# An attention layer and a routed mixture of experts on one core: the side work of the attention's 16 slots assigned anew

## The reference

```python
# layer 1: attention with 16 heads of 16, weights scaled by a "coherence" and mixed with a field
attn = softmax(q @ k.T / sqrt(16))
coh = sigmoid(tanh(concat(x, cond) @ Wc1.T + bc1) @ Wc2.T + bc2)
mod = attn * coh;  mod = mod / (mod.sum(-1) + 1e-8)
mod = 0.79 * mod + 0.21 * field          # one field weight for each key, from the condition
x = x + (mod @ v) @ Wout.T + bout
# layer 2: 8 experts of three products each, the best two for each row
gate = softmax(rmsnorm(x) @ wg_W + wg_b + cond @ gg_W + gg_b)
cw = the two largest gates of each row, zero elsewhere
x = x + sum over experts of cw * (W3 . relu(W2 . relu(W1 . x + b1) + b2) + b3)
```

## Time and profile before

| | us |
|---|---|
| median of 3 runs | 947.46 (939.85, 947.46, 947.79) |
| the profiled execution | 939.21 |
| its span | 937.1 |
| PE busy | 875.0 (93%) |
| DVE busy | 700.6 (75%) |
| ACT busy | 582.2 (62%) |
| POOL busy | 405.7 (43%) |

### The profile page before, as it was taken

The page is one execution under the profiler, slowest core; times in us unless marked ns, Lnnn a source line. Parts: engine busy times, 40 slices in busy tenths (PEclk is TensorE's granted clock), DMA queues, the critical chain, the costliest instruction groups (busy, mean ns, idle before and its releaser), DMA issues.

```text
span 937.1 us, 23130 instructions
## 1 busy us (share of the span) xinstructions
PE 875.0 (93%) x6806; PEld 513.9 (55%) x6807; DVE 700.6 (75%) x1678; ACT 582.2 (62%) x1256; POOL 405.7 (43%) x446
## 2 busy tenths in 40 slices
PE   5799999999999999998988889999999999999994
PEld 2233333333333333332321568888888888888873
DVE  7888889898889989898887578667855555555542
ACT  3267787887877788776577767644444444444441
POOL 4414345545656456552343436534642332223322
PEclk9899999999999999998796999999999999999998
DMA  6462261633616254360046489435643333333442
GB/s 220 114 105 71 50 115 55 108 98 88 126 60 107 93 102 89 82 129 5 20 148 220 145 222 254 85 54 107 125 78 47 57 52 53 46 48 58 69 45 24
DMA packets 109434, 88.39 MB, mean 94 GB/s; under 512 B 63816, under 2 KB 102088, under 8 KB 107024
## 3 DMA queue, kind: packets, MB, share of 16 engines
q1 hardware_dynamic: 95664, 68.05, 31.6%
q0 software_dynamic: 13296, 18.23, 11.7%
q10 hardware_dynamic: 384, 0.97, 0.3%
HBM read 45.01 MB, written 33.31 MB: 84 GB/s over the span
## 4 chain that ended last, share of the span: by engine, by line
PE 74%; DVE 9%; DMA 6%; ACT 5%; issue 3%; POOL 1%; SPq 1%; ACTq 0%; DVEq 0%; POOLq 0%
PE bank L1025 28%; PE bank L870 11%; PE bank L922 9%; PE bank L1041 9%; PE bank L857 8%; DVE mx L1290 4%; PE bank L846 4%; DMA raw<-in_we 3%; PE bank L928 2%; ACT arena L1173 2%; PE bank L980 1%; DVE arena L1596 1%; POOL arena L626 1%; DMA out<-y,y_dest 1%; ACT arena L1121 1%
## 5 line engine op out<-in xcount | busy, mean ns | idle before, releaser
L1290 DVE TENSOR_REDUCE mx<-bank 128x1 f32<-128x512 f32 x512 | 324.2, 682 | 40.8 <-PE bank L846 37.5
L1173 ACT ACTIVATE arena<-bank 128x512 f32<-128x512 f32 x512 | 277.5, 596 | 64.8 <-PE bank L857 63.6
L1209 ACT ACTIVATE hf<-bank,small 128x256 f32<-128x256 f32 (+1 forms) x312 | 133.5, 455 | 187.9 <-PE bank L1025 183.7
L725 POOL DMA_INDIRECT out<-y,y_dest x71 | 123.2, 1735 | 240.4 <-DVE y_dest L1577 212.4
L1025 PE MATMUL bank<-hh,arena 128*128 128x256 f16 (+1 forms) x1248 | 198.4, 264 | 0.0
L1558 DVE TENSOR_TENSOR hl<-hf,hh 128x256 f16<-128x256 f32 (+1 forms) x304 | 112.8, 396 | 99.0 <-ACT hh L1213 98.8
L846 PE MATMUL bank<-arena 48*128 48x512 f16 x512 | 170.4, 394 | 14.3 <-DVE mx L1290 12.3
L857 PE MATMUL bank<-arena 49*128 49x512 f16 x512 | 166.6, 398 | 12.6 <-ACT arena L1173 6.9
L1025 PE MATMUL bank<-hl,arena 128*128 128x256 f16 (+1 forms) x624 | 163.5, 263 | 0.0
L870 PE MATMUL bank<-arena 128*17 128x512 f32 x1024 | 142.5, 630 | 0.9 <-ACT arena L1173 0.9
L857 PEld LDWEIGHTS bank<-arena 49*128 49x128 f16 x512 | 38.9, 94 | 178.5 <-ACT arena L1173 150.2
(11 more groups left out here) (230 smaller groups left out, 987.9 us busy)
## 6 DMA issues: line engine op xcount, KB each, us to landing
raw<-in_we SPq DMA_DIRECT2D x16, 1024.0 KB, 5.3
arena<-parts_dram SPq DMA_DIRECT2D x84, 128.0 KB
parts_dram<-arena SPq DMA_DIRECT2D x64, 128.0 KB, 1.8
arena<-in_xT SPq DMA_DIRECT2D x8, 512.0 KB, 4.5
arena<-in_x SPq DMA_DIRECT2D x8, 512.0 KB, 6.3
out<-rows SPq DMA_DIRECT2D x8, 512.0 KB, 5.2
xs<-in_pads SPq DMA_DIRECT2D x9, 272.0 KB, 3.8
arena<-parts_dram SPq DMA_DIRECT2D x24, 64.0 KB, 2.8
```

The costliest lines, as they stand in the source:

```text
L725: pool.indirect_dma_start(out=out, out_offset=bass.IndirectOffsetOnAxis(ap=y_dest[:, par, s:s + 1], axis=0), in_=y[:, par, s, :], in_offse ...
L1173: nc.scalar.activation(pr[:, s % TT, n, :], b_bank[no % B_RING][:, :], ACT.Exp, scale=SCALE).then_inc(b_read, 1)
L1209: nc.scalar.activation(hf[which][:, m, 0:n], layer[which][m // 2][:, m % 2 * TS:m % 2 * TS + n], ACT.Relu, bias=bias[which][:, bass.ds(e, ...
L1290: V.tensor_reduce(mx[:, g % 2, c, s % TT:s % TT + 1], a_bank[no % A_RING][:, :], X, ALU.max).then_inc(a_read, 1)
```

## The change

Only tables and the places of calls change; every instruction stays.

- `at` 0 (the first half of the second turning) of a batch moves from slot 11 to slot 0 of the next batch (in the last batch, to slot 13).
- `v` 0 moves from slot 0 to slot 4, `v` 2 from 14 to 13, `vs` from 7 to 6 and GpSimd's `sum_values` from 6 to 5.
- `pj` 3 moves from slot 13 to 14; its write to DRAM from 15 to 16, ahead of the first stack read, which moves from slot 0 to 1.
- `split_x` moves from slot 4 to 1 on ScalarE and from 5 to 2 on GpSimd.
- `square_rows` 0 moves from slot 4 to 5. `send_high` moves from slots 8 and 9 to 6 and 9, `send_low` from 8 and 10 to 7 and 14, `targets` from 14 to 15.

```diff
 PLAN = {
-    0: [("coh", 0, 0), ("v", 0, 1)],
+    0: [("at", 0, -1), ("coh", 0, 0)],
...
-    4: [("op", 1, -1)],
+    4: [("op", 1, -1), ("v", 0, 1)],
     5: [("ot", 0, 0), ("op", 2, -1)],
-    6: [("op", 3, -1)],
-    7: [("vs", 0, 0), ("c1", 0, 1)],
+    6: [("op", 3, -1), ("vs", 0, 0)],
+    7: [("c1", 0, 1)],
...
-    11: [("at", 0, 0), ("v", 1, 1)],
+    11: [("v", 1, 1)],
     12: [("pj", 1, 2), ("count", 0, -1)],
-    13: [("ot", 2, 0), ("pj", 3, 2)],
-    14: [("v", 2, 1)],
+    13: [("ot", 2, 0), ("v", 2, 1)],
+    14: [("pj", 3, 2)],
...
-SENT_AT = {8: 0, 10: 1}
+SENT_HIGH_AT = {6: 0, 9: 1}
+SENT_AT = {7: 0, 14: 1}
+SQUARES_AT = {5: (0, 1), 6: (2,), 7: (3,)}
...
-STACKS_AT = {0: 0, 3: 1, 4: 2}
+STACKS_AT = {1: 0, 3: 1, 4: 2}
...
-PARTS_AT = (10, 12, 14, 15)
+PARTS_AT = (10, 12, 14, 16)
...
+    if s == FINAL + 13:
+        here.append(("at", 0, B - 1))
...
+            if at == PARTS_AT[3] - SLOTS and 0 <= b + 1 < B:
+                write_parts(3, b + 1)
...
-            if at in PARTS_AT and 0 <= b + 2 < B:
+            if at in PARTS_AT[:3] and 0 <= b + 2 < B:
...
-            if at == 5 and 0 < b + 2 < B:
+            if at == 2 and 0 < b + 2 < B:
                 split_x(b + 2)
-            if at == 6 and 0 <= b < B:
+            if at == 5 and 0 <= b < B:
                 sum_values(b)
...
-            if at == 14 and 0 <= b - 1 < B:
+            if at == 15 and 0 <= b - 1 < B:
                 targets(b - 1)
...
-            if 4 <= at < 8 and 0 <= b - 1 < B:
-                square_rows(at - 4, b - 1)
-            if at in (8, 9) and 0 <= b - 1 < B:
-                send_high(at - 8, b - 1)
+            if at in SQUARES_AT and 0 <= b - 1 < B:
+                for t in SQUARES_AT[at]:
+                    square_rows(t, b - 1)
+            if at in SENT_HIGH_AT and 0 <= b - 1 < B:
+                send_high(SENT_HIGH_AT[at], b - 1)
...
-            if at == 4 and 0 < b + 2 < B:
+            if at == 1 and 0 < b + 2 < B:
                 split_x(b + 2)
```

## The result

The changed kernel takes 967.6 us (median of 4 runs, 964.07 to 971.21) against 943.65 us of the kernel before in the same comparison: ratio 1.0253, 95% interval 1.0178 to 1.0329. The forecast was 951.9 in 935 to 960, with no change beyond 1% the likeliest. It is 24 us slower than the kernel before, and 16 over the forecast. The profiled execution took 971.21 us, its span is 969.1. In what follows medians take all runs, while ratios and their intervals leave out the runs of a slower state of the chip.

The account below looks back on a forecast made before the run. TensorE's own work was taken as the floor, so only its waits could be won. Batch 0 -2.2, batch 1 -1.1, batches 2 to 5 +4.8, batch 6 +2.9: +4.4 us on a median of 947.46, forecast 951.9, range 935 to 960.

Parts of the forecast that it names:

- The wait of `send_high`: Slot 6, batches 2 to 6: ScalarE waits 2.6 us for the last two scatters, TensorE stands 2.3 us.
- the stop as its own price: Sum, batches 2 to 6: TensorE's stop in slot 6 costs just its length, 2.3 us a batch.
- pushes its scatters of slots 3 and 4 into time in which it idles: GpSimd's split of x in slot 2 delays these scatters into its idle time; no cost in the sum.
- In the start `pj` 3 falls behind a small setup product; GpSimd is then still busy with `pj` 1, so nothing.: Start, ahead of slot 0: the later `pj` 3 costs nothing.
- ScalarE in slots 4 to 6, -1.52: Slots 4 to 6: moving the split of x and a square removes TensorE's whole wait, -1.52 us a batch.
- Slots 11 and 12, -0.65 with `at` 0's own 0.49: Slots 11 and 12: VectorE relieved of `send_low` and `at` 0's subtraction, -0.65 us a batch, `at` 0's 0.49 included.
- Slots 1 and 2, +0.6: Slots 1 and 2: `at` 0 in slot 0 delays the chain to `at` 1, +0.6 us a batch, ends 0 and 1.0.
- Batch 1, -1.1: Batch 1, without the new wait: -1.52 - 0.65 + 0.49 + 0.6 = -1.1 us.
- Batch 0, -2.2: Batch 0, which has no `at` 0 before it: -2.2 us.
- Batch 7, 0: Batch 7 and the experts, bound by VectorE and the weights: 0; no new wait taken.
- The rival on the slower side: Slot 4: late `pj` 3 write delays stack read and maxima's turning, store misses the border; 961 us, chance 0.14.
- The wait does not come: Slot 6: scatters land as issued or GpSimd leads ScalarE more, no wait; -7.1, 940.4 us, chance 0.20.

Follow-up runs that it names:

- experiment 1: Changed kernel with only the first `send_high` and the `send_low` behind it back from slots 6 and 7 to slot 8: 950.16 us, ratio 1.0055.
- experiment 2: Changed kernel with GpSimd's half of the split of x in slot 7, behind the scatters, instead of slot 2: 963.27 us, ratio 1.0192.
- experiment 9: Changed kernel with first send, `at` 0 and whole start back as before, GpSimd's split of x behind slot 4's scatters: 937.63 us, ratio 0.995.
- experiment 10: Same as experiment 9, but with the start of the changed kernel: 943.22 us, ratio 1.0009.
- experiment 13: Kernel of experiment 9 with only `pj` 3 of batch 0 moved behind the small setup product, as in the change: 940.5 us, ratio 0.9983.
- experiment 6: Kernel of experiment 5 with `at` 0 also back from slot 0 to slot 11: 943.84 us, ratio 1.0.
- experiment 5: Changed kernel with the edits of experiment 1 and experiment 3, and GpSimd's split of x back in slot 5: 947.6 us, ratio 1.0045.
- experiment 3: Changed kernel with the slots ahead of slot 0 as before, except the second batch's `pj` 3: 963.48 us, ratio 1.0223.
- experiment 4: Changed kernel with slot 6's sum over the values done five times over on TensorE in batches 2 to 6: 962.74 us, ratio 1.0213.
- experiment 8: Changed kernel with `v` 3 of batch 0 done six times, to fill TensorE's stop in the start: 969.28 us, ratio 1.0266.
- experiment 11: Kernel of experiment 1 with the eight stack reads moved behind the turning of the maxima of slot 6: 968.28 us, ratio 1.0259.

## Why the prediction was wrong

- **The wait of `send_high`** was right in place, cause and size: the earlier trace rows gave 2.3 us of TensorE and a slot 6 near 5.6; the trace has 5.55 to 5.59 in batches 4 to 6 against 3.37 without the wait, 2.2 us, and more in batches 2 (6.77) and 3 (5.72). The chain was right as well: it put the end of the last issue 1.06 us later than in batch 6 of the kernel before, 2.82 us after slot 6's border, and in batch 4 it is 2.84 after it. The Trainium skill, page "DMA: Bandwidth & Descriptors", section "Anatomy of one DMA — SWDGE (gpsimd) path", gives about 2.0 us plus the bytes over 436 GB/s for a DMA that GpSimd issues, by which a scatter of 128 rows of 1,088 bytes (272 numbers in f32) would take an estimated 2.3 us from its issue. The trace agrees, with 2.54 (321.22 to 323.76), but for batches 2 and 3, where it is 3.8 and 2.8.
- **The step that failed: the stop as its own price.** The term of the sum is 2.3 us in each of batches 2 to 6, 11.5 us: I costed the stop with the time it lasts and let TensorE go on at the old pace. The granted clock then fell to half in slot 7 in four of five batches, 1.85 us each in batches 3 to 5 (5.32 for 3.47) and 2.8 in batch 2: experiment 1 brings back 17.4 us, where slot 6's five stops make up some 12. Two more terms failed that stood at nothing, the next two.
- **GpSimd's split "pushes its scatters of slots 3 and 4 into time in which it idles"**: true of GpSimd, and I stopped there. I left out what SP's queue moves in that time. The later scatters meet the eight stack reads, and `pv`'s bank comes late to ScalarE in slot 4: 0.5 to 1.6 us a batch, 3.9 us in batches 2 to 5 by the slots of experiment 2.
- **"In the start `pj` 3 falls behind a small setup product; GpSimd is then still busy with `pj` 1, so nothing."** In the changed kernel GpSimd's half of it ended 0.7 us later (22.24 for 21.51), and the half clock fell on the score tiles; the new start costs 5.6 us by experiments 9 and 10. That the 0.7 us are the cause isn't shown: in experiment 13 they are 0.1, and slot 0 comes at 52.3 all the same. Which of the moves does it, and how, stays open.
- **ScalarE in slots 4 to 6, -1.52**: right in batch 1, where these slots take 3.54 + 3.33 + 3.37 = 10.24 us, against 10.57 in batch 4 before, though `v` 0 (0.79) and `vs` (0.59 in its row above) came in.
- **Slots 11 and 12, -0.65 with `at` 0's own 0.49**: 7.76 for 8.36, right in size, but experiment 6 shows that all of it is `at` 0; `send_low`, to which I gave half of VectorE's relief, is worth nothing there. **Slots 1 and 2, +0.6**: 7.16 for 6.52 in batch 1, but the size came right partly by luck. The chain that was to cost it ends with `at` 1 in slot 2, whose wait was to be near 0.9 us; it is 0.28 as before, and `at` 1 starts only 0.20 us later in its slot. `at` 0 accounts for 0.36 of it (experiments 5 and 6), the rest, by its place in slot 1, I put down to ScalarE's split of x, which was not tried.
- **Batch 1, -1.1**: -1.13. **Batch 0, -2.2**: no profile shows it. Batch 0 takes 60.6 in the changed kernel and 56.6 to 62.2 in experiments 1 to 4 and 8, 56.4 and 58.0 in the two profiles of the kernel before; its first part runs partly at half clock in every profile but one of these two. **Batch 7, 0**: 75.04 for 72.05, but the kernel before has 72.05 and 75.88 in its two profiles, with the half clock in different places; what of it is the change's stays open.
- **The rival on the slower side**, the late maxima, wasn't it: in the changed kernel no border of slot 4 waits for the stored row. "The wait does not come" gave 7 us, and without the wait the change is still slower (experiment 1); with the start, slot 4 and `at` 0 taken back too it is 0.5% faster (experiment 9).

The sum: 17.4 (experiment 1) + 3.9 (slot 4, experiment 2) + 5.6 (9 and 10) = 27 us, of which the prediction had 11.5. Measured are 24, so the rest of the change would win 3, where the prediction had 7; the 3 are a remainder, and experiment 9, with all three taken back, lies 3.5 us under the kernel before (937.63 for 941.14).

## What to carry to other kernels

A stop of TensorE, where it bounds, has two prices, its length and what the clock does after it; look at the granted clock of the slots behind each new wait. Here a stop of 2.1 to 2.2 us cost some 4.0 where the half clock followed it (slots 6 and 7 of batch 4 against experiment 1), and some 2.5 where it did not (batch 6). A step moved into idle time of its own engine's queue can still meet another queue's transfers there: list what the DMA engines move in the new place as well. Price the first hundred microseconds by themselves, and by many runs: an order that costs nothing in the steady batches cost 5.6 us there, while single profiles of one and the same start put slot 0 anywhere from 47.7 to 55.5 us.

## What the runs showed of the hardware

- TensorE's clock was at half level for part of the slot behind a stop of 1.89 to 4.67 us in 20 of 25 batches, and in that slot in none of 55 batches without the stop.
- Scatters from GpSimd and SP's reads moving together held up the hand-over from TensorE to ScalarE: in batch 4 of the changed kernel the last product of `pv` in slot 4 is over at 313.27 by its row, and the copy that waits for it starts at 314.58; with scatters and reads apart (experiments 2 and 11) slot 4 takes 3.54 to 3.59. By what way they do it no run here shows.
- One kernel's runs spread by up to 19 us (before: 934.73 to 953.38 in 29 runs), while a slot without half clock repeats within some hundredths from batch to batch and profile to profile (slot 6 of the kernel before: 3.24 or 3.25 us in batches 1 to 5 of both its profiles). A single profile tells a slot's length well and a kernel's time badly.
